# The attention stage of a two-block metaformer kernel: feature map in one VectorE pass, squares of x3 on GpSimd, clamp on ScalarE, other orders

## The reference, cut to what matters

```
def _feature_map(t):
    return jax.nn.elu(t) + 1.0
q = jnp.einsum('oc,bchw->bohw', q_w, x) + q_b[None, :, None, None]
Q = _feature_map(_to_seq(q))
Z = 1.0 / (jnp.einsum('nlhd,nhd->nlh', Q, K.sum(axis=1)) + EPS)
out = jnp.einsum('nlhd,nhdv,nlh->nlhv', Q, KV, Z) * S
out = jnp.einsum('oc,bchw->bohw', proj_w, out) + proj_b[None, :, None, None]
...
x = x + _L1_conv_ref(_ln_c(x), ...)          # x3
logits = jnp.einsum('bsd,ed->bse', _ln_t(x3_as_tokens), gate_w) + gate_b
vals, idx = jax.lax.top_k(softmax over tokens, K)     # K = 8 for each of 32 experts
```

## Time and profile before

| what | value |
|---|---|
| median of 3 runs | 1968.5 us |
| the profiled execution | 1974.39 us, of it the span 1972.3 us |
| attention stage in it | from about 1133 us (first load) to about 1750 us |
| PE, DVE, ACT, POOL busy over the whole span | 80%, 74%, 64%, 73% |
| the same from 1350 to 1450 us | 95.7%, 93.4%, 87.7%, 89.6% |
| granted PE clock from 1350 to 1450 us | 1.00 of full speed |

### The profile page before, as it was taken

One profiled execution on the slowest core, in us unless ns is written; L12 is line 12 of the kernel. 1 busy time (PEld: TensorE's weight loads), 2 busy tenths in 40 slices (PEclk: granted clock), 3 DMA queues, 4 the chain that ended last, 5 costly groups with the idle time before them and its releaser, 6 DMA issues. The chain is left out here.

```text
span 1972.3 us, 24751 instructions
## 1 busy us (share of the span) xinstructions
PE 1572.6 (80%) x5690; PEld 652.4 (33%) x5690; DVE 1461.2 (74%) x2373; ACT 1269.9 (64%) x2235; POOL 1438.2 (73%) x1070
## 2 busy tenths in 40 slices
PE   4899999999999972887884969999999999925100
PEld 1333333333333321455551613223222323205100
DVE  1689999999999973788886547999999999941000
ACT  2777777777777651787772468888888888720000
POOL 2999999999999970086776059988998898801570
PEclk8999999999999985999896979999999999955555
DMA  4588788888878656999994067888888887660011
GB/s 152 157 234 254 240 250 249 252 245 249 255 240 253 191 179 187 283 326 364 363 389 196 4 219 247 269 271 270 256 265 273 268 259 241 204 146 14 2 2 1
DMA packets 127392, 429.89 MB, mean 218 GB/s; under 512 B 59632, under 2 KB 64656, under 8 KB 82192
## 3 DMA queue, kind: packets, MB, share of 16 engines
q1 hardware_dynamic: 105568, 423.83, 68.0%
q10 hardware_dynamic: 18736, 4.29, 1.4%
q0 software_dynamic: 2944, 0.18, 0.1%
HBM read 257.93 MB, written 170.01 MB: 217 GB/s over the span
## 5 line engine op out<-in xcount | busy, mean ns | idle before, releaser
L454 ACT ACTIVATE tap_products<-xn,kk 128x512 f32<-128x512 f32 x384 | 275.2, 718 | 165.7 <-POOL x_and_products L485 159.9
L485 POOL TENSOR_TENSOR x_and_products<-tap_products,x_and_products 128x512 f32<-128x512 f32 x256 | 326.7, 1276 | 41.7 <-POOL x_and_products L485 3.5
L385 PE MATMUL pst<-xn,taps 128*128 128x512 f32 x768 | 351.6, 593 | 0.0
L1440 POOL TENSOR_SCALAR exp_q<-exp_q 128x512 f32<-128x512 f32 x128 | 201.4, 1573 | 117.8 <-ACT exp_q L1395 117.8
L910 DVE SCALAR_TENSOR_TENSOR pss<-region,bn,pss 128x256 f32<-128x256 f32 x432 | 196.5, 488 | 69.5 <-PE pss L814 67.7
L849 POOL TENSOR_TENSOR x_block<-x_block,region 128x2048 f32<-128x2048 f32 x28 | 155.2, 5543 | 116.5 <-ACT region L836 82.8
L543 DVE SCALAR_TENSOR_TENSOR pst<-xn,kk,pst 128x512 f32<-128x512 f32 x256 | 191.7, 749 | 61.9 <-PE pst L385 61.7
L385 PEld LDWEIGHTS pst<-xn,taps 128*128 128x128 f32 x768 | 145.4, 190 | 186.2 <-issue 186.0
L485 POOL TENSOR_TENSOR x_and_products<-tap_products,x_ring 128x512 f32<-128x512 f32 x128 | 164.2, 1283 | 20.2 <-ACT tap_products L454 20.2
L1454 POOL TENSOR_TENSOR q_z<-q_map,z_inv 128x512 f32<-128x512 f32 x128 | 163.7, 1279 | 7.1 <-issue 5.2
L425 ACT ACTIVATE sq<-x_ring 128x512 f32<-128x512 f32 x256 | 157.7, 622 | 16.1 <-POOL x_ring L492 10.1
(11 more groups left out here) (243 smaller groups left out, 2996.1 us busy)
## 6 DMA issues: line engine op xcount, KB each, us to landing
rstd_wide<-rstd_scratch SPq DMA_DIRECT2D x128, 512.0 KB, 7.2
x_ring<-in_x SPq DMA_DIRECT2D x32, 1024.0 KB, 5.2
x_scratch<-x_ring SPq DMA_DIRECT2D x32, 1024.0 KB, 4.3
xl_scratch<-wx SPq DMA_DIRECT2D x32, 1024.0 KB, 8.7
region<-xl_scratch SPq DMA_DIRECT2D x32, 1024.0 KB, 11.4
x_ring<-x_scratch SPq DMA_DIRECT2D x32, 1024.0 KB, 8.4
rstd_of_channels<-rstd_scratch SPq DMA_DIRECT2D x64, 512.0 KB, 6.2
x_transposed<-x_squares SPq DMA_DIRECT2D x64, 512.0 KB, 5.0
```

What stands on the lines that cost most here:

```text
L385: m = pe.matmul(wide(pst[g % 2]), taps[:, n * P:(n + 1) * P], tap_rows(g, t), start=(n == 0), stop=(n == len(PE_TAPS) - 1))
L454: act.activation(prod[:, n, :, :], tap_rows(g, t), ACT.Copy, scale=kk[:, t:t + 1]).then_inc(products, 1)
L485: pool.tensor_tensor(xr[:, g % XR, :], prod[:, n, :, :].rearrange("p r w -> p (r w)"), xr[:, g % XR, :] if n else x_tile(g), ALU.add).then ...
L1440: pool.tensor_scalar(e, e, 1.0, None, ALU.min).then_inc(clipped, 1)
```

## The change

- The feature map is written as max(q + bias + 1, min(exp(q + bias), 1)). DVE computes it in one instruction, `scalar_tensor_tensor`, from `query` and the clipped `exp_q`, with a per-partition scalar `qb1` = bias + 1 made once ahead of the loop. The instruction `relu_query` on DVE and the sum `map_query` on POOL go.
- `square_x3` moves from ACT to POOL, as a product of the tile with itself.
- The clamp of the variances moves from DVE to ACT, as a relu that reads PSUM, at the head of `rsqrt`.
- `rstd_to_experts` issues four transfers of two pieces each a block in place of eight of one piece.
- `query` gets four slots (two before), `exp_q` four (three), `q_map` four (six). The lags and the order of the calls within a step are other ones on every engine.

```
-            LOAD, SQ2, QUERY, QSCALE, QMAP, DENOM, BYZ, ATTEND, X3, SQ3, TURN = -6, 0, 7, 9, 11, 11, 13, 13, 13, 13, 14
-            STATS = (3, 18)
-            GATE, GSCALE, BEST, BEST_AT, EXPSUM = 23, 23, 25, 26, 29
+            LOAD, SQ2, QUERY, QSCALE, QMAP, DENOM, BYZ, ATTEND, X3, SQ3, TURN = -1, 6, 15, 16, 17, 18, 18, 20, 20, 20, 27
+            STATS = (10, 24)
+            QCLIP = 16
+            GATE, GSCALE, BEST, BEST_AT, EXPSUM = 30, 30, 33, 35, 37
...
-                            for i in range(2):
-                                sp.dma_start(rb4[rows, k % 2, i * TILE:(i + 1) * TILE],
-                                             r4_d[k, b, (2 * i + j) * TILE:(2 * i + j + 1) * TILE].partition_broadcast(E)
-                                             ).then_inc(rb4_loaded[k % 2], 16)
+                            sp.dma_start(rb4[rows, k % 2, :].rearrange("p (i n) -> p i n", n=TILE),
+                                         r4_d[k, b, :].rearrange("(i j n) -> j i n", j=2, n=TILE)[j].partition_broadcast(E)
+                                         ).then_inc(rb4_loaded[k % 2], 16)
...
+                    act.wait_ge(var_done, n + 1)
+                    if n:
+                        act.wait_ge(ln_done, n)
+                    act.activation(var[:, :], pse[:, :], ACT.Relu).then_inc(clamped, 1)
...
             def _(pool):
+                def square_x3(g):
+                    pool.wait_ge(x3_ready, g + 1)
+                    if g >= SQSLOTS[1]:
+                        pool.wait_ge(second_ready, round_of[1, (g - SQSLOTS[1]) // TPB] + 1)
+                    pool.tensor_tensor(sq[1][:, g % SQSLOTS[1], :], x_tile(g), x_tile(g), ALU.mult).then_inc(squared[1], 1)
...
-                def map_query(g):
-
-                    pool.wait_ge(clipped, g + 1)
-                    pool.wait_ge(relu_ready, g + 1)
-                    r = qm[:, g % QSLOTS, :]
-                    pool.tensor_tensor(r, eq[:, g % 3, :], r, ALU.add).then_inc(mapped, 1)
...
-                    if (g := tile_at(t, QMAP)) is not None:
+                    if (g := tile_at(t, SQ3)) is not None:
+                        square_x3(g)
+                    if (g := tile_at(t, QCLIP)) is not None:
                         clip_exp(g)
                     if (g := tile_at(t, BYZ)) is not None:
                         query_by_inverse(g)
-                    if (g := tile_at(t, QMAP)) is not None:
-                        map_query(g)
...
-                def clamp(l, k):
-                    n = round_of[l, k]
-                    dve.wait_ge(var_done, n + 1)
-                    if n:
-                        dve.wait_ge(ln_done, n)
-                    dve.tensor_scalar(var[:, :], pse[:, :], 0.0, None, ALU.max).then_inc(clamped, 1)
...
+                def map_query(g):
+
+                    dve.wait_ge(clipped, g + 1)
                     dve.wait_ge(q_scaled, g + 1)
                     if g >= QSLOTS:
                         dve.wait_ge(qz_ready, g - QSLOTS + 1)
                         dve.wait_ge(d_ready, g - QSLOTS + 1)
-                    dve.tensor_scalar(qm[:, g % QSLOTS, :], qs[:, g % 2, :], qb, 0.0, ALU.add, ALU.max).then_inc(relu_ready, 1)
+                    dve.scalar_tensor_tensor(out=qm[:, g % QSLOTS, :], in0=qs[:, g % QRING, :], scalar=qb1[:, 0:1],
+                                             in1=eq[:, g % 4, :], op0=ALU.add, op1=ALU.max).then_inc(mapped, 1)
```

More of the change, by code:

```diff
@@ L1144, in build_program @@
             rstd = sb("rstd3", [P, 2, TILE], F32, ph)
-            qs = sb("query", [P, 2, TILE], F32, ph)
-            eq = sb("exp_q", [P, 3, TILE], F32, ph)
+            qs = sb("query", [P, QRING, TILE], F32, ph)
+            eq = sb("exp_q", [P, 4, TILE], F32, ph)
             qm = sb("q_map", [P, QSLOTS, TILE], F32, ph)
+            qb1 = sb("q_bias_plus_1", [P, 1], F32, ph)
             lnd = sb("ln_d", [P, TILE], F32, ph)
@@ L1273, in _ @@
                 for t in range(LOAD, STEPS_D):
[L1274 to L1277, removed]
+                    if (k := block_at(t, STATS[1] + 3)) is not None:
+                        rstd_to_experts(k)
+                    if (k := block_at(t, LOAD)) is not None:
+                        load(k)
                     for l in range(2):
@@ L1280, in _ @@
                             rstd_to_dram(l, k)
+                    if (h := pair_at(t, TURN + 1)) is not None:
+                        store_xt(h)
+                    if (k := block_at(t, X3 + TPB)) is not None:
+                        store_x3(k)
                     if (k := block_at(t, STATS[0] + 3)) is not None:
                         rstd_to_channels(k)
[L1283 to L1286, removed]
                 for k in range(NBLK - SEMS, NBLK):
@@ L1343, in _ @@
                 for t in range(0, STEPS_D):
-                    if (g := tile_at(t, ATTEND)) is not None:
-                        attend(g)
-                    if (g := tile_at(t, DENOM)) is not None:
-                        denominator(g)
                     if (g := tile_at(t, QUERY)) is not None:
@@ L1351, in _ @@
                         gate(p)
+                    if (g := tile_at(t, DENOM)) is not None:
+                        denominator(g)
+                    if (g := tile_at(t, ATTEND)) is not None:
+                        attend(g)
                     for l in range(2):
@@ L1392, in exp_query @@
                     act.wait_ge(q_scaled, g + 1)
[L1393 to L1395 removed]
+                    if g >= 4:
+                        act.wait_ge(mapped, g - 3)
+                    act.activation(eq[:, g % 4, :], qs[:, g % QRING, :], ACT.Exp, bias=qb).then_inc(expq_ready, 1)
                 def log_denominator(g):
@@ L1523, in best_logits_at @@
                     dve.tensor_scalar(nm[:, k:k + 1], cand[:, k * K:k * K + 1], -1.0, None, ALU.mult).then_inc(neg_ready, 1)
+                dve.tensor_scalar(qb1[:, :], qb, 1.0, None, ALU.add).then_inc(prepared, 1)
+                dve.wait_ge(prepared, 1)
                 for t in range(0, STEPS_D):
-                    rounds = [(l, k) for l in range(2) if (k := block_at(t, STATS[l] + 1)) is not None]
                     if (g := tile_at(t, QSCALE)) is not None:
                         scale_query(g)
+                    rounds = [(l, k) for l in range(2) if (k := block_at(t, STATS[l] + 1)) is not None]
                     if (g := tile_at(t, TURN)) is not None:
                         turn_x3(g)
+                    for l, k in rounds:
+                        variance(l, k)
                     if (g := tile_at(t, X3)) is not None:
                         add_attention(g)
-                    for l, k in rounds:
-                        variance(l, k)
-                    if (g := tile_at(t, QSCALE)) is not None:
-                        relu_query(g)
-                    for l, k in rounds:
-                        clamp(l, k)
+                    if (g := tile_at(t, QMAP)) is not None:
+                        map_query(g)
                     if (p := pair_at(t, GSCALE)) is not None:
```

46 lines of the change are left out of this document (18 added, 28 removed).

## The result

The changed kernel took 1937.2 us (median of 4 runs, 1932.7 to 1939.5) against 1967.5 us of the kernel before on the same chip: ratio 0.9844, interval 0.9825 to 0.9862, some 30 us faster. The forecast was 8 us faster, and the time lies 0.8 us under the low end of the range (1938). The two profiled executions have spans of 1937.7 and 1972.3 us, 34.6 us apart.

| | before | after | difference | forecast |
|---|---|---|---|---|
| to the first x3 | 1167.0 | 1167.6 | +0.6 | 0 |
| first to last x3 | 559.1 | 528.3 | -30.8 | -5.2 |
| last x3 to last `neg_best` | 22.9 | 19.6 | -3.3 | -3 |
| from there to the end | 223.3 | 222.2 | -1.1 | 0 |

A forecast was written before the change was run, and what follows sets the result against it. The prediction saw a ring of waits with no engine full, then POOL as bound at 4.39 us a tile instead of 4.49. Gains of 5.2 us plus 3 in the tail make 8.2: 1968.5 to 1960 us, range 1938 to 2002.

The forecast's parts named there:

- POOL then has 3.94 us a tile, plus 0.45 for the map: 4.39.: POOL's clip 1.45, `q_z` 1.24 and square 1.25 us, plus 0.45 for the map's exclusion, set the new period.
- the square ... I take 1.25 us, with 1.24 and 1.49 as bounds: Price of the square moved to POOL, taken from the sum, a product of the same shape.
- Counted between 0.86 and 1.01, make 3.95 to 4.10; 4.05 taken.: PE's time a tile for three matmuls, half a gate and one statistics group, under POOL's 4.39 us.
- The exclusion: DVE's map, with two SBUF inputs, excludes POOL, ends 0.55 us after POOL's instruction and costs POOL 0.45 us.
- No exclusion: Rival, chance 0.09: the map runs beside POOL, PE's 4.05 us is the period, 43.5 us more gained: 1917.
- POOL gets in first: Rival, chance 0.08: POOL's square beats DVE's map behind x3, period 5.02 us, last x3 79 us later: 2044.
- The idle time stays: Rival, chance 0.21: the ring of waits closes elsewhere, POOL keeps 0.44 us idle a tile: 2016, half of it 1988.
- POOL's idle 0.44 us: POOL's idle time a tile before the change, mostly waiting for ACT's `exp_q`; the wait for `exp_q` was to go.
- the map's 0.45: What each map on DVE was to cost POOL a tile by exclusion; bounds 0.17 and 0.55 us.
- The tail: After the last x3, four transfers halve SP's 6.38 us issue; 3 us gained, bounds 0 and 4.75.

The follow-up runs named there:

- x1: Changed kernel with POOL's square made a product of the tile with a constant tile of ones; 1931.8 us, ratio 0.9807, first to last x3 552.6 us.
- x2: Changed kernel with DVE's map replaced by a transpose of `exp_q`, one input in SBUF; ratio 0.9804, first to last x3 524.8 us.
- x8: Changed kernel with DVE's variance put between x3 and the map instead of ahead of x3; ratio 1.0051, first to last x3 571.1 us.
- x5: Changed kernel with PE's gate moved behind attend, next to the statistics; ratio 1.0046, first to last x3 568.7 us.
- x15: x7 with POOL's old order inside a step (clip, `q_z`, sum of the map); 2274 us, ratio 1.1562, first to last x3 855.6 us.
- x7: Changed kernel's orders, lags, rings and four transfers, with the work on the engines as before the change; ratio 0.9846, first to last x3 528.3 us.
- x16: Kernel before the change with only the four transfers for the experts' factors in place of eight; ratio 0.9995.
- x9: Changed kernel with PE's old order (attend, denominator, query, gate); ratio 0.9848, first to last x3 533.9 us.
- x12: Moved work and rings of four, with lags, orders and transfers of the kernel before; 2473 us, ratio 1.2551, first to last x3 1060.6 us.

## Why the prediction was wrong

- **"POOL then has 3.94 us a tile, plus 0.45 for the map: 4.39."** This step failed, by one term: "the square ... I take 1.25 us, with 1.24 and 1.49 as bounds". It is 1.04, less 0.03, so POOL has 4.15. I had no bound below the nearest row, though the row was for two tiles and this product reads one. With the term as I priced it (x1) the tile takes 4.39 us exactly.
- **"Counted between 0.86 and 1.01, make 3.95 to 4.10; 4.05 taken."** The second mis-sized term: it is 4.205, above even my upper end. I priced the three wide products at the 0.86 of wide behind wide, where four of the six in a pair take 0.95 to 0.97, 0.39 us a pair; gate and statistics (1.01 and 1.85) lay within what I had counted. DVE and ACT I had priced by their busy share; PE's, 0.957 x 4.49 = 4.30 us, would have warned me. Since POOL fell under it, this term became the bound. 127 x (4.39 - 4.205) = 23.5 us is nearly all of the 25.6 by which the stretch was missed.
- **The exclusion** was right: 0.55 us behind `q_z`, 0.44 us on POOL. *No exclusion* is refuted, and its 43 us were never there to win: x2 removes the exclusion and gains 3.5, since PE holds the tile.
- **"POOL gets in first"** did not happen in the order of the change, the map standing right behind x3; x8 brings it about with one instruction between. The price there is 43 us of stretch, not 79: it strikes one tile in two, and 0.30 us of it is covered. Of the 1.00 us by which the map is late there, 0.59 is the variance itself.
- **"The idle time stays"** is refuted for the change (POOL at 99.1%), but the rings of x5 and x15 show that it was the live danger: 40 us of stretch more than the changed kernel, 327 more than x7. I weighed it by spare time of engines; it hangs on what stands between a release and its use.
- **What the gain is owed to.** My sum had POOL's idle 0.44 us go and the map's 0.45 come. That the idle time goes with the orders was right; that the moved work has a price or a worth in the time was not: x7 without it has the same stretch. The gain comes from the orders with their lags and rings, which took away the waits of the earlier trace rows, and ends at PE's sum. With the old orders the moved work costs 504 us. So the direction was forecast rightly, by a bound (POOL's 4.39) that was not there.
- **The tail** came to 3.3 us against 3, right in size by luck: x16 gives the transfers 0.7 of it.

## What to carry to other kernels

When a wait that closes a ring is opened, the next bound is a sum over one engine: add up that engine from start to start, pair of neighbours by pair of neighbours, in the new order. Before moving a call within a step, walk each ring from release to use and count what work covers it; here 0.30 us of cover decided 40 us. And test order and moved work apart, since a change that has both can owe all to one. And when a bound is priced from a row of another shape, ask what a cheaper price would make the bound.

## What the runs showed of the hardware

- POOL's product of a 128x512 f32 tile with itself took 1.04 us, that of two tiles 1.27.
- A DVE instruction with two inputs in SBUF that comes while a POOL instruction runs ended 0.54 to 0.55 us behind it, and POOL's next took 0.44 to 0.45 us longer, both for products and for the clip (1.93 us in x8 against 1.48). The relu with one input cost 0.17.
- PE's pitch for 512 columns f32 was 0.86 us between two products with 128x128 weights and 0.95 to 0.97 where the neighbour's weights are 32 or 64 wide. The width is not the only way to it: in x9 an attend between two wide products took 0.95 (1409.65 to 1410.60 us), and its weights were loaded only when `q_z` was there (weight loads of PE in x9):

```profile
1409.63 0.30 PEld L1334 LDWEIGHTS ps_attended<-q_z,mT 128*128 128x128 f32 x2 [0.65 <-POOL q_z L1451]
```

- The granted clock of PE was 1.00 (2.4 GHz) in the middle of the stage before and after, with PE 96 to 100% busy. In x12 its mean was 0.88 with PE 255.65 of 400 us busy. Behind 2.82 us of waiting a denominator took 2.07 us there, where others take 1.12, and from 1407 to 1410 us the granted clock was 0.50, the lower level of 1.2 GHz (windows, then timeline of PE). The denominator and the query behind it took 1.87 and 1.71 us from start to start, where 0.96 and 0.95 are usual.

```profile
1250.00:1650.00 400.00, 255.65 (x752) 68.57 (x754) 192.73 (x285) 186.63 (x305) 195.75 (x141) 0.88 0.43 140
1407.00:1410.00 3.00, 3.00 (x4) 1.04 (x4) 2.29 (x4) 0.98 (x2) 3.00 (x3) 0.50 1.02 216
```

```profile
1406.87 2.07 PE L1328 MATMUL ps_denominator<-q_map,dT 128*128 128x512 f32 x2 [2.82 <-DVE q_map L1484]
```
